# The first layer's mixture moves from VectorE to ScalarE and GpSimd, with fewer idle turns on TensorE

## What is computed

```
xn  = layernorm(x)
# graph part: three diffusion steps over a normalised adjacency matrix
h   = xn @ W + b
out = w[0] * h
cur = h
for i in range(3):
    cur = adj @ cur
    out = out + w[i + 1] * cur
gnn = relu(out)
# attention part: ends with an output projection and a norm with a weights' row gamma
o   = attention(xn) @ w_out.T
mix = (o - mean(o)) * rsqrt(var(o) + eps) * gamma
x   = x + gnn + mix
x   = x + experts(layernorm(x))      # 16 experts, top 2
```

## Time and profile before

| what | before |
| --- | --- |
| median of 3 runs | 223.85 us |
| lowest and highest run | 223.84 and 232.37 us |
| the profiled execution's own time | 222.05 us |
| its span | 220.3 us |
| mean granted clock of TensorE | 0.991 |

### The profile page before, as it was taken

The page is one execution under the profiler, slowest core; times in us unless marked ns, Lnnn a source line. Parts: engine busy times, 40 slices in busy tenths (PEclk is TensorE's granted clock), DMA queues, the critical chain, the costliest instruction groups (busy, mean ns, idle before and its releaser), DMA issues.

```text
span 220.3 us, 2936 instructions
## 1 busy us (share of the span) xinstructions
PE 210.9 (96%) x1031; PEld 142.9 (65%) x1031; DVE 141.2 (64%) x416; ACT 63.2 (29%) x148; POOL 22.1 (10%) x36
## 2 busy tenths in 40 slices
PE   7899999999999999999999999999959999999994
PEld 5685547666589988744646786478724564798641
DVE  3899999968998441432629259796934779653302
ACT  2804584322221012100101169730633321103100
POOL 4860010000111000000150000000300001200000
PEclk9999999999999999999999999999999999999969
DMA  5999799935050500000199000000000000000002
GB/s 164 355 394 358 238 404 416 412 118 176 1 190 4 190 0 3 0 0 0 44 297 405 18 0 1 3 0 0 0 0 3 0 0 0 1 3 0 0 0 95
DMA packets 8957, 23.65 MB, mean 107 GB/s; under 512 B 2408, under 2 KB 2408, under 8 KB 8944
## 3 DMA queue, kind: packets, MB, share of 16 engines
q1 hardware_dynamic: 8656, 23.42, 29.0%
q10 hardware_dynamic: 288, 0.07, 0.1%
HBM read 22.95 MB, written 0.52 MB: 107 GB/s over the span
## 4 chain that ended last, share of the span: by engine, by line
PE 84%; DVE 11%; issue 1%; DMA 1%; ACT 1%; POOL 0%; DVEq 0%
PE bank L1180 17%; PE bank L1154 12%; PE bank L1284 10%; PE bank L1272 10%; PE bank L1229 5%; PE bank L1315 4%; PE bank L1191 3%; PE bank L1235 3%; DVE ring L784 3%; PE bank L1329 2%; PE bank L1236 2%; PE bank L1168 2%; DVE ring L787 2%; PE bank L1220 2%; DMA xa<-in_x 1%
## 5 line engine op out<-in xcount | busy, mean ns | idle before, releaser
L1180 PE MATMUL bank<-raw,xT 128*128 128x512 f32 x88 | 39.3, 595 | 0.0
L1180 PEld LDWEIGHTS bank<-raw,xT 128*128 128x128 f32 x88 | 16.2, 190 | 18.3 <-issue 18.2
L301 POOL TENSOR_TENSOR rstd<-veps,minus_half 128x1 f32<-128x1 f32 x14 | 9.2, 660 | 153.2 <-DVE veps L561 111.1
L1315 PE MATMUL bank<-iota_bf 128*128 128x256 bf16 x155 | 21.5, 286 | 1.6 <-DVE iota_bf L760 1.6
L1284 PE MATMUL bank<-raw,ring 128*128 128x512 f32 x48 | 22.7, 633 | 0.0
L1272 PE MATMUL bank<-xT,raw 128*128 128x256 f32 x96 | 22.1, 384 | 0.0
L784 DVE TENSOR_SCALAR ring<-iota_bf,edges,radix 128x128 bf16<-128x128 bf16 x64 | 20.8, 376 | 0.0
L1315 PEld LDWEIGHTS bank<-iota_bf 128*128 128x128 bf16 x155 | 16.1, 107 | 5.2 <-DVE iota_bf L760 1.6
L1272 PEld LDWEIGHTS bank<-xT,raw 128*128 128x128 f32 x96 | 17.8, 190 | 2.3
L1284 PEld LDWEIGHTS bank<-raw,ring 128*128 128x128 f32 x48 | 9.6, 202 | 12.0 <-issue 11.6
L1191 PE MATMUL bank<-xT,raw 128*128 128x256 f32 x64 | 14.6, 382 | 0.2 <-issue 0.2
(11 more groups left out here) (256 smaller groups left out, 331.6 us busy)
## 6 DMA issues: line engine op xcount, KB each, us to landing
raw<-in_up SPq DMA_DIRECT2D x6, 512.0 KB, 10.6
raw<-in_down SPq DMA_DIRECT2D x6, 512.0 KB, 13.8
raw<-in_k SPq DMA_DIRECT2D x4, 512.0 KB, 5.5
raw<-in_q SPq DMA_DIRECT2D x4, 512.0 KB, 6.3
raw<-in_v SPq DMA_DIRECT2D x4, 512.0 KB, 6.9
raw<-in_out SPq DMA_DIRECT2D x4, 512.0 KB, 6.9
raw<-in_gat SPq DMA_DIRECT2D x4, 512.0 KB, 9.5
raw<-in_gnn SPq DMA_DIRECT2D x2, 512.0 KB, 10.0
```

Of the source, the lines that this page charges most:

```text
L1180: ins = mm(bank[banks[t]][:, :], xT_at(c, t), w.at(c), start=c == 0, stop=c == C - 1)
L1315: mm(half(b, 0), iota_bf[:, 0:P], iota_bf[:, :], start=True, stop=True)
```

## The change

VectorE keeps mean and variance of the projected tiles, and adds one 128x1 operation, the negated mean. ScalarE takes the rest of the arithmetic that reads PSUM: it centres the tile with that negated mean as bias, and then scales it by the reciprocal root. GpSimd then multiplies by the row `gamma0` and adds x, in its own order: root of tile 0, two operations on tile 0, root of tile 1, two operations on tile 1, and only then the roots of the next norm. The first term of the diffusion sum moves to ScalarE too, ahead of the diffusion. `residual(t)` now waits for its own tile of `mixed`; before, VectorE waited for both. On TensorE the idle turns between the third step and the transposes of tile 1 go from 29 to 11, and one `attention_weights` block moves behind the transposes of tile 0.

```diff
@@ -157,6 +157,7 @@
         junk = [g[:, :, :].rearrange("p t (a n) -> p (t a) n", a=2) for g in (g_a, g_b)]
         attblk = sb("attblk", [P, C, 2 * H])
         stats = sb("stats", [P, T, 6])
+        minus_mean = sb("minus_mean", [P, T])
         mv = sb("mv", [P, T, 2])
         veps = sb("veps", [P, T])
         rstd = sb("rstd", [P, T])
@@ -218,7 +219,8 @@
             ["dst_full", "z_ready", "max_full", "shifted", "exp_ready", "weight_ready"])
         agg_full, y_ready, elu_exp, out_ready, stored = (sem(n) for n in
             ["agg_full", "y_ready", "elu_exp", "out_ready", "stored"])
-        degree_ready = sem("degree_ready")
+        degree_ready, diffused_ready = sem("degree_ready"), sem("diffused_ready")
+        mean_ready, mix_centred, mix_scaled = sem("mean_ready"), sem("mix_centred"), sem("mix_scaled")
         kinv_ready, sign_loaded = sem("kinv_ready"), sem("sign_loaded")
         xn_less_one, sum_full = sem("xn_less_one"), sem("sum_full")
 
@@ -318,7 +320,13 @@
                                              att1[:, a, :].unsqueeze(2).broadcast_to([P, C, H]), ALU.mult))
             nc.gpsimd.memset(hx[:, :, :, HD:HD + 1], 1.0).then_inc(consts, 1)
 
-            roots(1)
+            for t in range(T):
+                pool.wait_ge(var_ready, T + t + 1)
+                nc.gpsimd.tensor_tensor(rstd[:, t:t + 1], veps[:, t:t + 1], minus_half[:, t:t + 1], ALU.pow)\
+                    .then_inc(rstd_ready, 1)
+                pool.wait_ge(mix_scaled, t + 1)
+                then(nc.gpsimd.tensor_tensor(mixed[:, t, :], mixed[:, t, :], row["gamma0"], ALU.mult))
+                nc.gpsimd.tensor_tensor(mixed[:, t, :], mixed[:, t, :], xa[:, t, :], ALU.add).then_inc(mix_ready, 1)
             roots(2)
             roots(3)
             pool.wait_ge(xT_full, 6)
@@ -422,9 +430,25 @@
             yT_part(0, (4, 5))
             act.wait_ge(linked_ready, 2)
             copy(count[:, :, :], bank[3][:, :].rearrange("p (c n) -> p c n", c=T)).then_inc(count_ready, 1)
+            act.wait_ge(small_in, SMALLS)
+            for t in range(T):
+                nc.scalar.activation(diffused[:, t, :], hr[:, t, :], ACT.Copy, scale=diffusion[:, 0:1])\
+                    .then_inc(diffused_ready, 1)
             act.wait_ge(degree_ready, 1)
+            def mixture(t):
+                act.wait_ge(o_full, t + 1)
+                act.wait_ge(mean_ready, t + 1)
+                nc.scalar.activation(mixed[:, t, :], bank[t][:, :], ACT.Identity, bias=minus_mean[:, t:t + 1])\
+                    .then_inc(mix_centred, 1)
+                act.wait_ge(rstd_ready, T + t + 1)
+                act.wait_ge(mix_centred, t + 1)
+                nc.scalar.activation(mixed[:, t, :], mixed[:, t, :], ACT.Copy, scale=rstd[:, t:t + 1])\
+                    .then_inc(mix_scaled, 1)
+
             diffuse(0, (2, 7))
+            mixture(0)
             diffuse(1, (3, 4))
+            mixture(1)
             xT_part(1, 4)
             act.wait_ge(wa_full, 1)
             copy(wa[:, :, 0:2 * H], bank[6][:, 0:C * A2].rearrange("p (c n) -> p c n", c=C)[:, :, 0:2 * H])
@@ -855,8 +879,6 @@
                 dve.wait_ge(cur_rounded, t + 1)
                 V.tensor_tensor(cur_lo[:, 0, t, :], hr[:, t, :], cur_hi[:, 0, t, :].bitcast(f32), ALU.subtract)\
                     .then_inc(cur_ready, 1)
-            for t in range(T):
-                go(V.tensor_scalar(diffused[:, t, :], hr[:, t, :], diffusion[:, 0:1], None, ALU.mult))
             dve.wait_ge(degree_ready, 1)
             for i in range(STEPS):
                 go(V.tensor_scalar(degree_w[:, i, :], degree[:, :], diffusion[:, i + 1:i + 2], None, ALU.mult))
@@ -882,23 +904,19 @@
             def mixture(t):
                 dve.wait_ge(o_full, t + 1)
                 variance(1, t, bank[t][:, :])
-                go(V.scalar_tensor_tensor(mixed[:, t, :], bank[t][:, :], mv[:, t, 0:1], row["gamma0"],
-                                          ALU.subtract, ALU.mult))
-                settle()
-                dve.wait_ge(rstd_ready, T + t + 1)
-                V.scalar_tensor_tensor(mixed[:, t, :], mixed[:, t, :], rstd[:, t:t + 1], xa[:, t, :],
-                                       ALU.mult, ALU.add).then_inc(mix_ready, 1)
+                V.tensor_scalar(minus_mean[:, t:t + 1], mv[:, t, 0:1], -1.0, None, ALU.mult).then_inc(mean_ready, 1)
 
             mixture(0)
+            dve.wait_ge(diffused_ready, T)
             diffuse(0)
             mixture(1)
             dve.wait_ge(step_read, 2)
             diffuse(1)
             dve.wait_ge(step_read, 4)
-            dve.wait_ge(mix_ready, 2)
 
             def residual(t):
                 dve.wait_ge(step_read, 4 + t + 1)
+                dve.wait_ge(mix_ready, t + 1)
                 go(V.scalar_tensor_tensor(xb[:, t, :], diffused[:, t, :], 0.0, mixed[:, t, :], ALU.max, ALU.add))
                 settle()
                 variance(2, t, xb[:, t, :])
@@ -1389,15 +1407,15 @@
             pe.wait_ge(step_read, 2)
             diffuse(2, (2, 7))
             attention_weights(0, 6, 0)
-            idle_turns(5, 7)
+            idle_turns(5, 3)
             attention_weights(0, 6, 1)
-            idle_turns(5, 7)
-            attention_weights(0, 6, 2)
             idle_turns(5, 3)
             pe.wait_ge(step_read, 4)
             xT_made(1, xn, (4, 5), (0,))
+            attention_weights(0, 6, 2)
+            idle_turns(5, 3)
             attention_weights(0, 6, 3).then_inc(wa_full, 1)
-            idle_turns(5, 12)
+            idle_turns(5, 2)
             xT_made(1, xn, (4, 5), (1,))
             pe.wait_ge(mix_ready, 2)
             pe.wait_ge(step_read, 6)
```

## The result

| what | before | after |
| --- | --- | --- |
| median | 223.84 us (4 runs) | 229.44 us (4 runs, 228.83 to 230.07) |
| ratio | | 1.0272, 95% interval 1.0211 to 1.0334 |
| span of the profiled execution | 220.3 us | 227.1 us |
| mean granted clock of TensorE | 0.991 | 0.962 |

The change makes the kernel 2.7% slower.

What follows compares the result with a forecast made beforehand. TensorE, busy 96% of the span, was taken to bound the kernel. An earlier third diffusion step gained 0.49, GpSimd's hold on VectorE's residual gave back 0.52, leaving nothing: 223.8 us, range 222.2 to 226.2.

Steps and rivals of the forecast that it cites:

- Removed work costs nothing: VectorE's moved `diffused` and first-tile mixture operations only shortened waits: worth nothing; ScalarE's two added operations hide in idle time.
- `both_lo` and step 2 come 0.49 earlier: VectorE's `both_lo` (code's `cur_lo`) pair ends 0.6 earlier; TensorE's third diffusion step begins at 63.48, not 63.97.
- The sum: Main case's total, measured at the start of TensorE's second-tile transposes: nothing left, 0.03 later, time 223.8.
- 0.49 gained, 0.52 given back: Main case's balance: third diffusion step 0.49 earlier, then 0.52 lost by the second-tile transposes; nothing left.
- GpSimd's operations, 1.39 each: GpSimd's second-tile multiply and addition, 128x512 with two SBUF inputs: 1.39 each, half of 2.78 for 128x1024.
- The residual is held: VectorE's first residual waits for GpSimd's second-tile addition until 66.83 and starts 0.76 later; main case, chance 0.40.
- T1's data at 72.90: Second normed tile, needed by TensorE's second-tile transposes (T1), ready at 72.90, 0.76 later; the transposes start at 72.95.
- the stretch: Time from first matmul of diffusion step 1 to first of the up projection: 15.95 before, 19.38 after.
- TensorE goes on without loss: Main case, chance 0.40: no added clock fall on TensorE between third diffusion step and second-tile transposes.
- the fall of the clock: Rival, chance 0.22: TensorE's clock falls once between 65.6 and second-tile transposes; 225.7 with GpSimd's hold, 224.5 without.
- The price of a fall, 1.90: Cost of one TensorE clock fall, from 16 matmuls near 209 us: 8.77 - 6.87 = 1.90 lost.
- A fall vanishes at 209: Rival, chance 0.05: the existing TensorE clock fall at 209 disappears as timing shifts; 1.9 less, about 221.9.

## Why the prediction was wrong

- **Removed work costs nothing, `both_lo` and step 2 come 0.49 earlier:** right. Step 2 came 0.35 earlier in an execution that was 0.21 later, so 0.56. The sum's "0.49 gained, 0.52 given back" is short for 1.22 gained (0.49, and 0.73 of turns no longer waited for) and 1.25 given back; the result, 0.03 later, is the same.
- **GpSimd's operations, 1.39 each:** measured 1.26 to 1.30. The estimate from the Trainium skill's figure ("GPSIMD Engine Reference", section 3.1), a quarter of it, was 1.12, too little; half of the row of 128x1024 was too much.
- **The residual is held:** right, to 66.87 where I said 66.83 (66.66 without the later start); the lead of the addition was 0.09 where I said 0.16. The run with the fill showed the reverse order, GpSimd held instead, at 1.64 for 1.26. The Trainium skill, "SBUF — State Buffer", section "Who interferes with whom", calls the shared port pair an exclusive lock; both traces agree, with 1.72 and 1.64.
- **T1's data at 72.90:** 73.13, or 72.92 without the later start. The number is right in part by luck: the held residual ended 0.33 earlier than in the sum (67.42, less 0.21, for 67.54), and the stall of 0.43 ahead of the first normed tile, where the sum had 0.08, took that back. With the turns of before put back, 224.01 was measured where 223.8 was predicted, though the stretch grew by 0.28 where the sum had 0.03.
- **TensorE goes on without loss:** this step failed. I gave the fall of the clock a chance of 0.22, and the runs with thin filling ahead of the first transposes in the changed kernel all have it (after, and the runs with few turns ahead). In the changed kernel it fell behind 2.4 us of light blocks and turns and a wait of 2.34. My evidence against it was a single microsecond at 161 with TensorE busy 0.12, from one execution. At that very place the clock did fall in six of the eleven traces, the changed kernel's among them: the eight matmuls that took 1.89 at 163.59 before took 3.24 at 170.43 after. A clock that stayed up there once showed nothing.
- **The price of a fall, 1.90:** the mis-sized term, and the reason why the range missed too. I took it from a fall inside a dense stretch, which ended while the same matmuls ran on (the last down projection, 8.83 with it and 7.13 without, so 1.70). This one lasted 10.2 us, with light work behind it until 79.00, and cost 19.38 - 16.23 = 3.15 up to the up projection and 1.5 behind it, against the same mixture with enough turns: 4.65 in all, where the sum had 1.90.
- **A fall vanishes at 209:** it did, for 1.7; but two came at 123 and 171. Such falls stand in every trace here, one to three in an execution.

## What to carry to other kernels

Idle turns that fill a wait cost nothing here, and without ten of them the clock fell; before they are cut, ask what TensorE would do without them. Cut them only down to the moment when the data come: 24 in place of 29 shortened the stretch of the kernel before by 0.45, in one trace. And a fall of the clock is priced by what follows it: in dense work it cost 1.7 here, ahead of a light stretch 4.7. One stretch that stayed at full clock in one execution is no evidence that it always does.

## What the runs showed of the hardware

One thing I had not expected. In the four traces with 6 turns ahead of the first transposes and the moved mixture, the clock stayed down for 10.2 to 13.7 us, and 4.2 us of idle turns at half speed did not end it; it came back 3.1 to 4.6 us into the up projection each time. Why is open. And one thing the runs bear out: of VectorE's residual and GpSimd's addition, which both read two tiles in SBUF, the one that starts second pays. 0.09 of lead made the residual 1.03 longer; with a 0.2 fill ahead of the addition, the residual led by 0.18 and the addition became 0.38 longer instead.
